# Attention logits of two graph layers kept in their PSUM bank: leaky ReLU in place, running maximum and subtraction from PSUM

## The chip, the cores and the metric

The kernel runs on one core of one Trainium2 chip, as one program. The metric is the device time of one execution in microseconds (us). Its engines are PE (TensorE, matrix products), DVE (VectorE), ACT (ScalarE), POOL (GpSimd) and SP (SyncE), each with an instruction queue of its own that it works off in order; they meet only at semaphores.

## What is computed

The reference is a graph network over 6250 nodes and 106250 edges, sorted by destination, in float32: a layer with a message sum, one with a mean, a GATv2 attention layer with a feed-forward part, and a block of two GAT layers (4 heads of 32 channels, then 1 head of 128). The change touches only the edge work of the last two:

```
def _gat_conv(x, edge_index, W, att_src, att_dst, bias, heads, out_ch, concat):
    h = (x @ W).reshape(N, heads, out_ch)
    a_src = jnp.einsum('nhc,hc->nh', h, att_src)
    a_dst = jnp.einsum('nhc,hc->nh', h, att_dst)
    e = a_src[src] + a_dst[dst]
    e = jnp.where(e > 0, e, NEG_SLOPE * e)          # NEG_SLOPE = 0.2
    m = jax.ops.segment_max(e, dst, num_segments=N)
    e = jnp.exp(e - m[dst])
    s = jax.ops.segment_sum(e, dst, num_segments=N)
    alpha = e / (s[dst] + 1e-16)
    out = jax.ops.segment_sum(h[src] * alpha[:, :, None], dst, num_segments=N)
```

## The kernel before, in words

The three attention layers run through one function, `soft_sweep`, called with layer 2 (GATv2), 3 (first GAT layer, H = 4 heads) and 4 (second GAT layer, H = 1). In it `full` is true for layer 2 alone; what stands under `not full` is layers 3 and 4, which are the fourth and fifth graph layers of the network. The edges are padded to G = 208 groups of GE = 512 edges (four pieces of 128). Four groups make a batch (BATCH = 4), so a layer has 52 batches. In a batch the logits stand as lanes: one partition for each head and group, L = 4H, so 16 partitions by 512 edges in layer 3 and 4 by 512 in layer 4.

What happens to a batch, in order:

- POOL (L1766) gathers the source rows of each piece with one indirect DMA: 832 in a layer, in a plain unrolled loop. It waits only for the message of 16 groups before (AROUND = 16). Each reads its 128 row numbers from the SBUF tile `sources`.
- ACT (L1780) takes the source parts of the logits from the gathered rows; PE sums destination parts (`dst_logits`, L1864) and source parts (`src_logits`, L1870) in `lane_bank`, one of two PSUM banks by the batch's parity.
- ACT (L1822) copies `lane_bank` to the SBUF tile `lanes`.
- DVE, `running_max`: L1980 makes the leaky ReLU, max(0.2 x bank, lanes), into `lanes`. L1983 is the forward running maximum, a scan over `starts` (added; a large negative number where a new destination begins) and the logits. L1987 takes its end, and L1989 scans backward over `starts` and `running`.
- DVE, `carry_on` and, one step later, `shift_lanes`: the maximum is carried across groups by way of PE (L1897, L1913); L2010 joins it into `running`, and L2012 subtracts `running` from the logits into `lanes`.
- ACT (L1810) takes the exponential; PE (L1920) turns the weights round into `weights_bank`; DVE (L2021) multiplies rows by weights; PE (L1880) scatters the messages with one-hot matrices into a window of 64 nodes, which DVE adds to the sums (L1972, L1974).

`sweep16` writes out the same list of steps for every engine, 16 groups to a loop body, and `t.back(k)` is the group k steps behind: a batch's weights are used LAG = 7 steps after its last group's first step began. A wait `wait_ge(sem, n)` holds the engine until the semaphore has reached n; `g.uses(BATCH)` is the number of the batch of group g, from one. On PE, the wait on `weights_lane` before L1920 stands in the step of `t.back(BATCH + 2)`, and the wait on `leaky` that the change replaces stands in `dst_logits`, in front of the first write to a `lane_bank` (j == 1).

Of the kernel before, what the change touches and what calls it, by code (L numbers as in the profile page):

```python
# [21 lines left out]
ALU = mybir.AluOpType  # L22
# [10 lines left out]
GE = TPG * P  # L33
# [8 lines left out]
BATCH = 4  # L42
# [8 lines left out]
AROUND = 16  # L51
NEG = -3.0e38
# [9 lines left out]
def sems(nc, phase, *names, **slots):  # L62

    lists = {n: [nc.alloc_semaphore(f"{phase}_{n}{k}") for k in range(count)] for n, count in slots.items()}
    return named(**{n: nc.alloc_semaphore(f"{phase}_{n}") for n in names}, **lists)
# [8 lines left out]
def settle(eng):  # L74

    eng.nop(nofuse=True)
# [1549 lines left out]
def soft_sweep(nc, io, sb, layer):  # L1626
# [3 lines left out]
    full = layer == 2  # L1630
# [12 lines left out]
    s = sems(nc, phase, *names, gathered=AROUND, attr=AHEAD, dst_rows=DST, onehotT=4, onehot=4)  # L1643

    with ExitStack() as ctx:
        def tile(name, shape, dt=F32):
            return ctx.enter_context(nc.sbuf_tensor(f"{phase}_{name}", shape, dt))[:]
# [6 lines left out]
        starts = tile("starts", [L, GE + 1])  # L1654
        cont = tile("cont", [L, GE])
        lanes = tile("lanes", [L, GE])
        running = tile("running", [L, GE])
# [20 lines left out]
        lane_bank = [sb.psum[0:L, 2 if full else k, :] for k in range(2)]  # L1678
# [20 lines left out]
        def pair(g):  # L1699
            return g.slot(8) // 2  # L1700

        with nc.Block() as block:  # L1702
# [129 lines left out]
            def _(pe):  # L1832
# [22 lines left out]
                def dst_logits(g):  # L1855
                    j = g.slot(BATCH)
                    pe.wait_ge(s.dst_rows[j], g.uses(BATCH, 16))
                    if g.slot(2) == 0:
                        return
                    pe.wait_ge(s.onehotT[pair(g)], g.uses(8, 16))  # L1860
                    if j == 1 and g.back(AROUND + 1).exists():
                        pe.wait_ge(s.leaky, g.back(AROUND + 1).uses(BATCH))
                    settle(pe)
                    pe.matmul(lane_bank[g.half()], dst_cols[:, j // 2], onehotT[:, pair(g)], start=j == 1, stop=False).then_inc(s.edge_term, 2)  # L1864

# [24 lines left out]
                def step(t):  # L1890
                    if t.exists():
                        (edge_terms if full else dst_logits)(t)
# [42 lines left out]
            def _(v):  # L1935
# [40 lines left out]
                def running_max(g):  # L1976
                    n = g.uses(BATCH)
                    v.wait_ge(s.lanes_out, n)
                    if not full:
                        v.scalar_tensor_tensor(lanes, lane_bank[g.half()], 0.2, lanes, ALU.mult, ALU.max).then_inc(s.leaky, 1)  # L1980
                        v.wait_ge(s.leaky, n)
                    v.wait_ge(s.starts_in, g.uses(BATCH, 16))
                    v.tensor_tensor_scan(running, starts[:, 0:GE], lanes, NEG, ALU.add, ALU.max).then_inc(s.running, 1)  # L1983
                    v.wait_ge(s.running, n)
                    if g.back(BATCH).exists():
                        v.wait_ge(s.carry_psum, g.back(BATCH).uses(BATCH))
                    v.tensor_scalar(fend, mask, running[:, GE - 1:GE], None, ALU.mult).then_inc(s.fend, 1)  # L1987
                    v.wait_ge(s.fend, n)
                    v.tensor_tensor_scan(running[:, ::-1], starts[:, GE:0:-1], running[:, ::-1], NEG, ALU.add, ALU.max).then_inc(s.backward, 1)  # L1989
# [13 lines left out]
                def shift_lanes(g):  # L2003
                    n = g.uses(BATCH)
                    v.wait_ge(s.init_psum, n)
                    v.tensor_copy(init, init_bank).then_inc(s.init, 1)
                    v.wait_ge(s.init, n)
                    v.wait_ge(s.backward, n)
                    v.wait_ge(s.cont_in, g.uses(BATCH, 16))
                    v.scalar_tensor_tensor(running, cont, init, running, ALU.add, ALU.max).then_inc(s.maxima, 1)  # L2010
                    v.wait_ge(s.maxima, n)
                    v.tensor_tensor(lanes, lanes, running, ALU.subtract).then_inc(s.shifted, 1)  # L2012
                    if g.back(BATCH).exists():
                        v.wait_ge(s.factor, g.back(BATCH).uses(BATCH))
                    v.tensor_scalar(growth, init, running[:, 0:1], 0.0, ALU.subtract, ALU.min).then_inc(s.factor_log, 1)
# [10 lines left out]
                def step(t):  # L2026
                    g = t.back(1)
                    if g.exists() and full:
                        v.wait_ge(s.z, g.times(1, 1))
                        v.scalar_tensor_tensor(z[:, g.slot(2)], z[:, g.slot(2)], 0.2, z[:, g.slot(2)], ALU.mult, ALU.max).then_inc(s.leaky, 1)  # L2030
                    g = t.back(LAG)
                    if g.closes(0):
                        q = g.half()
                        v.wait_ge(s.factor_psum, g.uses(BATCH))
                        v.tensor_copy(factor_of[:, q], factor_bank).then_inc(s.factor_out, 1)
                        v.tensor_copy(factor_head[:, q], factor_head_bank).then_inc(s.factor_out, 1)
                    if t.back(LAG + 1).exists():
                        add(t, t.back(LAG + 1))
                    if g.exists():
                        weigh(g)  # L2040
                    if t.back(BATCH + 1).closes(0):
                        running_max(t.back(BATCH + 1))
                    if t.back(BATCH + 2).closes(0):
                        shift_lanes(t.back(BATCH + 2))
                    g = t
                    if g.exists() and full:
                        v.wait_ge(s.edge_term, g.times(1, 1))
                        v.wait_ge(s.rows_out, g.times(1, 1))
                        v.tensor_tensor(z[:, g.slot(2)], term_bank, z[:, g.slot(2)], ALU.add).then_inc(s.z, 1)
                    if t.back(BATCH + 1).closes(0):  # L2050
                        carry_on(t.back(BATCH + 1))

                    if nodes:
                        nodes.dve_steps(v, t)
# [786 lines left out]
```

## Time and profile before

| | us |
|---|---|
| median of three runs (lowest, highest) | 6062.57 (6051.43, 6064.77) |
| the profiled execution | 6063.81 |
| its span in the trace | 6061.7 |
| PE busy | 4558.7 |
| POOL busy | 4033.9 |
| DVE busy | 2673.3 |
| ACT busy | 1391.0 |
| first and last gather of layer 3 issued at | 3799.8 and 4880.0 |
| first and last gather of layer 4 issued at | 4943.0 and 6008.9 |

The three runs lie within 13.3 us, 0.2% of the time. All positions are microseconds from the start of the span. The two layers of the change take the stretch from about 3800 to the end.

### The profile page before, as it was taken

The page shows a single profiled execution, that of the slowest core. Times are in us where ns is not written, and L with a number is a line of the kernel's source. Part 1 is how long each engine was busy: PE and PEld are TensorE (multiplying, and loading weights), DVE is VectorE, ACT ScalarE, POOL GpSimd, SP SyncE. Part 2 cuts the span into 40 slices and gives each one's busy share as a digit, 9 for nine tenths or more (in the row PEclk, how much of TensorE's full clock was granted, in tenths as well). Part 3 has the DMA queues.
Part 4 walks back from the last instruction along what each step waited for, and adds up shares of the span by engine and source line. Part 5 has one row for each costly group of instructions (what it writes and reads, how often), then busy time and mean ns, then how long its engine had stood idle before and what let it go on. Part 6 is the DMA issues. An engine that isn't in the chain of part 4 may idle for free. (4 is left out here: it accounts for less than half of the span.)

```text
span 6061.7 us, 88001 instructions
## 1 busy us (share of the span) xinstructions
PE 4558.7 (75%) x19879; PEld 2993.3 (49%) x19879; DVE 2673.3 (44%) x8236; ACT 1391.0 (23%) x4039; POOL 4033.9 (67%) x4164
## 2 busy tenths in 40 slices
PE   3788888647777776999999877577777756776666
PEld 2777777535565563444444455344444434444443
DVE  3222222221111113777777644455555545555555
ACT  2111111221222221222222255122222211222121
POOL 2777777447777775777777400777777747777775
PEclk9999999985555556999999967666676756667666
DMA  4333333244444443555555300445545524444442
GB/s 121 105 105 105 104 104 105 67 137 104 114 115 113 113 105 102 165 165 163 166 164 165 112 10 13 99 107 111 110 110 110 110 66 104 109 105 108 107 107 75
DMA packets 561737, 663.45 MB, mean 109 GB/s; under 512 B 197133, under 2 KB 392590, under 8 KB 560639
## 3 DMA queue, kind: packets, MB, share of 16 engines
q1 hardware_dynamic: 428351, 385.27, 21.5%
q0 software_dynamic: 133120, 275.45, 19.9%
q14 instruction: 199, 1.63, 0.1%
q8 instruction: 67, 1.10, 0.1%
HBM read 580.89 MB, written 86.19 MB: 110 GB/s over the span
## 5 line engine op out<-in xcount | busy, mean ns | idle before, releaser
L1766 POOL DMA_INDIRECT soft_rows<-table,sources x2496 | 2457.7, 985 | 1248.2 <-issue 1243.9
L1880 PE MATMUL psum<-soft_message,soft_onehot 128*64 128x136 f32 (+2 forms) x4992 | 948.0, 350 | 373.6 <-DVE soft_message L2021 200.0
L1880 PEld LDWEIGHTS psum<-soft_message,soft_onehot 128*64 128x64 f32 x4992 | 753.7, 177 | 805.9 <-issue 600.0
L1399 POOL DMA_INDIRECT sum_rows<-table,sources x832 | 785.4, 944 | 373.5 <-issue 369.8
L1069 POOL DMA_INDIRECT term_rows<-table,sources x832 | 790.7, 950 | 354.1 <-issue 354.1
L1806 ACT ACTIVATE soft_window<-psum 64x136 f32<-64x136 f32 (+2 forms) x624 | 171.5, 275 | 1885.1 <-PE psum L1880 1885.1
L1100 PE MATMUL psum<-term_onehot,term_term 128*128 128x64 f32 x1664 | 403.7, 424 | 188.5 <-DVE sums L1152 178.9
L1441 PE MATMUL psum<-sum_onehot,sum_rows 128*128 128x64 f32 x1664 | 358.0, 389 | 221.0 <-DMA sum_rows<-table,sources 220.1
L1100 PEld LDWEIGHTS psum<-term_onehot,term_term 128*128 128x128 f32 x1664 | 370.5, 328 | 242.1 <-issue 241.9
L1441 PEld LDWEIGHTS psum<-sum_onehot,sum_rows 128*128 128x128 f32 x1664 | 341.5, 302 | 274.7 <-issue 270.5
L1146 DVE TENSOR_TENSOR term_term<-psum,term_rows 128x512 f32<-128x512 f32 x208 | 143.8, 691 | 753.1 <-issue 371.1
L1972 DVE TENSOR_TENSOR sums<-sums,psum 128x64 f32 x624 | 136.7, 219 | 763.8 <-PE psum L1888 752.9
L1090 PE MATMUL psum<-L_We,term_attrs 64*128 64x128 f32 x1664 | 430.5, 437 | 8.9 <-DMA term_attrs<-in_ea64T 8.9
L2021 DVE TENSOR_TENSOR soft_message<-soft_rows,psum 128x512 f32<-128x512 f32 x624 | 417.8, 670 | 0.2 <-issue 0.2
L1090 PEld LDWEIGHTS psum<-L_We,term_attrs 64*128 64x128 f32 x1664 | 369.9, 325 | 57.1 <-issue 28.7
L1864 PE MATMUL psum<-soft_onehotT,soft_dst_cols 128*16 128x512 f32 (+1 forms) x416 | 321.9, 869 | 54.6 <-DMA soft_dst_cols<-adst 54.6
L1078 ACT ACTIVATE term_term<-term_term 128x512 f32<-128x512 f32 x208 | 130.9, 630 | 905.0 <-DVE term_term L1146 905.0
L1887 PEld LDWEIGHTS psum<-ident,soft_window 64*128 64x128 f32 x624 | 94.3, 151 | 462.6 <-issue 462.6
L1418 ACT ACTIVATE sum_flat<-psum 64x512 f32<-64x512 f32 x208 | 122.9, 591 | 825.7 <-PE psum L1431 822.1
L1480 DVE TENSOR_TENSOR sums<-sums,psum 128x64 f32 x208 | 46.1, 222 | 581.8 <-PE psum L1442 577.3
L1887 PE MATMUL psum<-ident,soft_window 64*128 64x64 f32 x624 | 182.0, 292 | 158.9 <-ACT soft_window L1806 158.4
L1846 PE MATMUL psum<-soft_onehotT,soft_dst_rows 64*128 64x512 f32 x416 | 235.9, 647 | 0.0
(239 smaller groups left out, 6576.6 us busy)
## 6 DMA issues: line engine op xcount, KB each, us to landing
soft_onehotT<-onehotsT SPq DMA_DIRECT2D x312, 256.0 KB
soft_onehot<-onehots SPq DMA_DIRECT2D x624, 128.0 KB
soft_attrs<-in_ea128T SPq DMA_DIRECT2D x208, 256.0 KB
soft_rows<-table,sources POOLq DMA_INDIRECT x2496
term_attrs<-in_ea64T SPq DMA_DIRECT2D x208, 128.0 KB
onehots<-term_onehot SPq DMA_DIRECT2D x208, 128.0 KB
sum_onehot<-onehots SPq DMA_DIRECT2D x208, 128.0 KB
onehotsT<-sum_flat SPq DMA_DIRECT2D x208, 128.0 KB
```

The lines of the kernel that those rows point to most:

```text
L1069: pool.indirect_dma_start(rows[:, k, t, :], None, io.table0[0:NCH * CN], bass.IndirectOffsetOnAxis(sb.sources[:, g * TPG + t:g * TPG + t + ...
L1090: last = pe.matmul(term_bank[g.slot(4)][:, piece(b)], attrs[:, g.slot(AHEAD), piece(b)], sb.L0_We, start=True, stop=True)
L1100: last = pe.matmul(window[q], term[:, g.slot(4), b, :], onehot[:, g.slot(8), b], start=b == 0, stop=b == TPG - 1)
L1399: pool.indirect_dma_start(rows[:, k, t, :], None, io.table1[0:NCH * CN], bass.IndirectOffsetOnAxis(sb.sources[:, g * TPG + t:g * TPG + t + ...
L1441: pe.matmul(window[q], rows[:, g.slot(AROUND), b, 0:D], onehot[:, k, b], start=b == 0, stop=b == TPG - 1)
L1766: pool.indirect_dma_start(rows[:, k, t, :], None, table[0:NCH * CN], bass.IndirectOffsetOnAxis(sb.sources[:, g * TPG + t:g * TPG + t + 1], ...
L1806: act.activation(window, window_bank, ACT.Copy).then_inc(s.window_copied, 1)
L1846: pe.matmul(term_bank, dst_rows[side(g), k], onehotT[side(g), pair(g)], start=False, stop=True).then_inc(s.edge_term, 1)
L1864: pe.matmul(lane_bank[g.half()], dst_cols[:, j // 2], onehotT[:, pair(g)], start=j == 1, stop=False).then_inc(s.edge_term, 2)
L1880: last = pe.matmul(window_bank, onehot[:, k, b], message[:, g.slot(2), b, :], start=b == 0, stop=b == TPG - 1)
L1887: pe.transpose(window_T[:, 0:W], window[:, 0:D], sb.ident[0:W, 0:W])
L2021: v.tensor_tensor(message[:, g.slot(2), :, 0:D].rearrange("p t (h c) -> p t h c", h=H), rows[:, g.slot(AROUND), :, 0:D].rearrange("p t (h ...
```

## The change

Three DVE instructions of a batch change their operands in layers 3 and 4, and one PE wait is put on another semaphore. Layer 2 is issued as before.

- L1980 writes its result over its PSUM input, `lane_bank`, in place of the SBUF tile `lanes`, which it still reads as its second input.
- L1983 reads the logits from `lane_bank` in place of `lanes`; `starts` stays in SBUF.
- L2012 reads the logits from `lane_bank` in place of `lanes`; `running` stays in SBUF, and so does its output.
- The bank is now read until the subtraction. `dst_logits` waits, before it writes to it anew, for the subtraction (`shifted`) of the batch two before, where it waited for the leaky ReLU of the batch four before.

```
-                    if j == 1 and g.back(AROUND + 1).exists():
-                        pe.wait_ge(s.leaky, g.back(AROUND + 1).uses(BATCH))
+                    if j == 1 and g.back(2 * BATCH).exists():
+                        pe.wait_ge(s.shifted, g.back(2 * BATCH).uses(BATCH))
...
+                    logits = lanes if full else lane_bank[g.half()]
                     if not full:
-                        v.scalar_tensor_tensor(lanes, lane_bank[g.half()], 0.2, lanes, ALU.mult, ALU.max).then_inc(s.leaky, 1)
+                        v.scalar_tensor_tensor(logits, logits, 0.2, lanes, ALU.mult, ALU.max).then_inc(s.leaky, 1)
                         v.wait_ge(s.leaky, n)
                     v.wait_ge(s.starts_in, g.uses(BATCH, 16))
-                    v.tensor_tensor_scan(running, starts[:, 0:GE], lanes, NEG, ALU.add, ALU.max).then_inc(s.running, 1)
+                    v.tensor_tensor_scan(running, starts[:, 0:GE], logits, NEG, ALU.add, ALU.max).then_inc(s.running, 1)
...
-                    v.tensor_tensor(lanes, lanes, running, ALU.subtract).then_inc(s.shifted, 1)
+                    v.tensor_tensor(lanes, lanes if full else lane_bank[g.half()], running, ALU.subtract).then_inc(s.shifted, 1)
```

## Rows read from the trace of the kernel before

**Rows 1.** The page, part 1: busy us (share of the span) and instructions
```profile
PE 4558.7 (75%) x19879; PEld 2993.3 (49%) x19879; DVE 2673.3 (44%) x8236; ACT 1391.0 (23%) x4039; POOL 4033.9 (67%) x4164
```

**Rows 2.** The page, part 4: the chain that ended last, by engine
```profile
POOL 13%; issue 4%; PE 0%; DVE 0%; ACT 0%; DMA 0%; POOLq 0%; DVEq 0%; ACTq 0%
```

**Rows 3.** Busy time of L1766 in layers 3 and 4: stretch, us, POOL busy (instructions)
```profile
core 0: us, POOL busy (x), PEclk, DMA share, GB/s
3795.00:4885.00 1090.00, 827.81 (x832) 0.66 0.48 108
4940.00:6011.00 1071.00, 813.65 (x832) 0.68 0.42 106
```

**Rows 4.** Line L1766, first of layer 3, then of layer 4: ns min/median/max, idle before it
```profile
L1766 POOL DMA_INDIRECT soft_rows<-table,sources x832: 940/944/1841, 3799.8 to 4880.0; - x167
...
  DVE soft_message L2021: 0.6, 2
...
L1766 POOL DMA_INDIRECT soft_rows<-table,sources x832: 940/944/1835, 4943.0 to 6008.9; - x167
...
  issue: 315.3, 832
```

**Rows 5.** DVE instructions of a batch by shape: busy us, mean ns, idle before
```profile
L2021 DVE TENSOR_TENSOR soft_message<-soft_rows,psum 128x512 f32<-128x512 f32 x624 | 417.8, 670 | 0.2 <-issue 0.2
L2030 DVE SCALAR_TENSOR_TENSOR soft_z<-soft_z 128x512 f32<-128x512 f32 x208 | 142.8, 687 | 31.0 <-issue 26.1
L1989 DVE TENSOR_TENSOR_SCAN soft_running<-soft_starts,soft_running 16x512 f32<-16x512 f32 x52 | 63.0, 1212 | 1.8
L1983 DVE TENSOR_TENSOR_SCAN soft_running<-soft_starts,soft_lanes 16x512 f32<-16x512 f32 x52 | 63.0, 1212 | 5.2 <-DMA soft_starts<-lane_starts 0.3
L2012 DVE TENSOR_TENSOR soft_lanes<-soft_lanes,soft_running 16x512 f32<-16x512 f32 x52 | 35.3, 679 | 1.8
L1980 DVE SCALAR_TENSOR_TENSOR soft_lanes<-psum,soft_lanes 16x512 f32<-16x512 f32 x52 | 35.0, 672 | 12.5 <-ACT soft_lanes L1822 12.5
```

**Rows 6.** Timeline, one batch of layer 3: start us, us, engine, line [idle before]
```profile
4079.64 0.67 DVE L1980 SCALAR_TENSOR_TENSOR soft_lanes<-psum,soft_lanes 16x512 f32<-16x512 f32 x1
...
4080.35 1.21 DVE L1983 TENSOR_TENSOR_SCAN soft_running<-soft_starts,soft_lanes 16x512 f32<-16x512 f32 x1
4080.52 1.79 POOL L1766 DMA_INDIRECT soft_rows<-table,sources  x1 [0.30 <-issue]
...
4081.84 1.21 DVE L1989 TENSOR_TENSOR_SCAN soft_running<-soft_starts,soft_running 16x512 f32<-16x512 f32 x1
4082.62 1.19 POOL L1766 DMA_INDIRECT soft_rows<-table,sources  x1 [0.31 <-issue]
...
4085.10 0.74 DVE L2010 SCALAR_TENSOR_TENSOR soft_running<-soft_cont,soft_init,soft_running 16x512 f32<-16x512 f32 x1
4085.37 1.29 POOL L1766 DMA_INDIRECT soft_rows<-table,sources  x1 [0.30 <-issue]
4085.87 0.68 DVE L2012 TENSOR_TENSOR soft_lanes<-soft_lanes,soft_running 16x512 f32<-16x512 f32 x1
```

**Rows 7.** Timeline, two batches of layer 4, the same columns
```profile
5013.65 1.21 DVE L1983 TENSOR_TENSOR_SCAN soft_running<-soft_starts,soft_lanes 4x512 f32<-4x512 f32 x1
5013.78 1.83 POOL L1766 DMA_INDIRECT soft_rows<-table,sources  x1 [0.30 <-issue]
...
5198.71 0.94 POOL L1766 DMA_INDIRECT soft_rows<-table,sources  x1 [0.30 <-issue]
5198.74 1.23 DVE L1983 TENSOR_TENSOR_SCAN soft_running<-soft_starts,soft_lanes 4x512 f32<-4x512 f32 x1
5199.96 0.95 POOL L1766 DMA_INDIRECT soft_rows<-table,sources  x1 [0.30 <-issue]
5200.25 1.21 DVE L1989 TENSOR_TENSOR_SCAN soft_running<-soft_starts,soft_running 4x512 f32<-4x512 f32 x1
5201.22 1.00 POOL L1766 DMA_INDIRECT soft_rows<-table,sources  x1 [0.30 <-issue]
```

## The prediction

> **What bounds the kernel now.** I began with the page's busy line: PE has most (75%), DVE less than half, POOL two thirds [rows 1]. That line mixes nine stages, so I went to the chain that ended last. It is POOL's: 13% of the span, with the sequencer's issue time as the only other share over 0% [rows 2]. Then line L1766 by layer. In layer 4 POOL issues 832 gathers from 4943.0 to 6008.9 and stands idle 315.3 us before them, all of it "issue", most of it in the fixed 0.30 us between two gathers; in layer 3 only 0.6 us of its idle time ends at another engine (DVE's message) [rows 4, 6]. So layers 3 and 4 last as long as POOL takes to issue: nothing that PE, ACT or DVE saves is worth anything there unless POOL gets faster by it. The reader is to see in rows 4 that the median gather takes 944 ns and the longest 1841 and 1835. At 944 ns, 832 take 785.4 us; they took 827.8 and 813.7 [rows 3]. POOL loses 42.4 us in layer 3 and 28.2 us in layer 4, 70.6 us together. The change can only be worth a part of that, or add to it.
>
> **Where POOL loses it.** The timeline with POOL and DVE side by side answers this. A gather that starts at 4080.52 takes 1.79 instead of 0.94, held by 0.85; the scan L1983 runs from 4080.35 to 4081.56, 1.04 after the gather's start. The next one is held 0.25, and L1989 ends 0.43 after its start. At 5013.78 it is 0.89 held and 1.08 to the scan's end, at 5201.22 0.06 and 0.24 [rows 6, 7]. The difference is 0.18 to 0.19 each time: a gather has one moment, 0.185 us after its start, at which it can't go on while such a DVE instruction runs, and it waits for that instruction's end. Call it the gather's read. Under L2010 the wait lasts 0.06 longer than the instruction (held 0.35, end at 0.47) [rows 6]. A read up to 0.16 us after a scan's start still slips through (5198.71), one 0.32 after it is held (5013.78) [rows 7]; I take 0.24 for the edge, with those two as its bounds.
>
> I went through all gathers and DVE instructions of the stretch from 3840 in this way. L1983 holds 75 of them, 26.5 us in total; L1989 101, 23.9 us; L2010 101, 18.6 us. That is 69.0 of the 70.6 us. These have two tensor inputs in SBUF. Reads that fall into L2021 (198 of them, one input in PSUM) or L1980 (52, one in PSUM) are not held at all. L2012 has two SBUF inputs but holds none: L2010 ends 0.03 before it starts and has just let a read through, and the next comes 1.2 us later, when L2012 is over [rows 6].
>
> The Trainium skill has this rule (SBUF — State Buffer, Who interferes with whom): a DVE instruction with two SBUF inputs contends with a GpSimd instruction that reads SBUF, one with at most one SBUF input does not. The held gathers agree. It also says that whoever comes second is blocked, DVE included; here the scans last 1212 ns in the mean whether or not they meet a gather, so that half is not seen.
>
> **The change, part by part.**
>
> *L1983 reads the logits from PSUM.* It keeps one SBUF input, as L2021 and L1980 have, so I take it that it no longer holds POOL. Its 26.5 us do not come back, though. Reads are 0.94 + 0.30 = 1.245 us apart, and L1989 starts 1.49 after L1983 [rows 6]. Say a read falls r after L1983's start. Before: held until 1.21, its next read is at 1.21 + 1.245 = 2.455, inside L1989 (1.49 to 2.70), held 0.25; in total 2.70 - 1.245 - r. After: it passes, the next read is at r + 1.245, inside L1989, held until 2.70: again 2.70 - 1.245 - r. The hold only moves from the first scan to the second. The exception is an r so small that r + 1.245 falls before L1989's edge, 1.49 + 0.24 = 1.73, so r under 0.49: then that read passes, the next at r + 2.49 comes after L1989's end, and the batch saves nearly all. Between the edge at 0.24 and 0.49 I find 12 of 104 batches, the first at 4080.52 (0.85 and 0.25 held, [rows 6]) and the last at 5013.78 (0.89 held, [rows 7]); ten of them in layer 3. Each saves its two holds, 1.0 to 1.15, and on the average 0.1 more at L2010. Laid over every batch's own positions, this gives 41.1 us of holds before and 29.3 after in layer 3, 28.5 and 26.0 in layer 4: 11.8 + 2.5 = 14.3 us saved. Check: in layer 3 the r are spread evenly over 1.245, so (0.49 - 0.24)/1.245 = 20% of 52 batches, 10.4 by 1.15 = 12.0. In layer 4 they cluster: most scans begin 0.03 to 0.5 after a gather's start, as at 5198.74, so few have a small positive r. With the edge at 0.16 the window ends at 0.41 and has 6 batches (7 us), with 0.32 it ends at 0.57 and has 16 (19 us): 7 to 19.
>
> *The durations.* They matter only through the position of L1989 and L2010 against the reads. With an input in PSUM the same kinds take 670 (L2021) and 672 (L1980) ns, all in SBUF 679 (L2012) and 687 (L2030) [rows 5]. So reading PSUM costs between -15 and 0 ns; a scan with a large PSUM input isn't in the trace, nor is any DVE write to PSUM. Bounds for these: 0.02 to 0.05 less each, from those pairs, and at the other end a second pass over 512 elements if reading and writing one bank exclude each other, which I put at half a scan's 1212 ns, 0.6 us. I take 0 to -0.05, as the PSUM rows lie there. With everything 0.05 earlier the positions give 30.5 and 23.5, a saving of 15.6; 0.1 later 25.8 and 31.1, 12.7.
>
> The Trainium skill speaks against the change here (VectorE: DVE Perf Modes, on the TRN2 errata): its fixed cost is 120 cycles from PSUM and 58 from SBUF. With L1983 longer by that difference, an estimate of 0.065 us at the page's 0.96 GHz, the saving would be 12 us. The rows show no such cost [rows 5].
>
> *L1980 writes to PSUM, L2012 reads from it.* L1980 held nothing and holds nothing. L2012 held nothing, so freeing it brings 0. Should L2010 stop standing in front of it, its place is worth no more than what L2010 takes now, 18.6 us. ACT still copies the bank first, so no instruction goes or comes on any queue.
>
> *The PE wait.* It asks for the subtraction of the batch two before, later than the old one. But PE has waited on `weights_lane` of the same batch three steps earlier (t.back(6) at step 4b - 2, this at 4b + 1), and ACT issues that only after `shifted`. So it is met when PE arrives, cost 0. If it were not, all of PE's scatters stand behind it; they have a gather's lead of 16 groups before POOL waits, so it would cost nothing on POOL either until PE were some 80 us late (16 groups of 1066/208 us).
>
> *Ends.* After the last gather of each layer some 53 to 58 us drain through all engines, with one such DVE chain in it: 0.1 us at most.
>
> **Sum.** 6063.8 (profiled execution) - 14.3 = 6049.5; against the median, 6062.6 - 14.3 = 6048.3. What no change looks like here is about 0.2%, 12 us.
>
> **Rivals.**
> 1. *The scan holds POOL still*, because the scan form itself takes the way to SBUF. For it: no scan with a PSUM input of size is in the trace. Against: L2010 and L1980 are one kind of instruction, and it is the place of the inputs that divides them. Time 6062.6, give or take 5 for the shift.
> 2. *The hold is gone and nothing takes its place*: if the positions move so that reads fall beside L1989. The whole 26.5 us: 6036. Against: L1989 holds a read that falls anywhere in 0.97 of every 1.245 us; only a shift of L1989 against the reads in most batches does it.
> 3. *Slower: writing over its own PSUM input makes L1980 and L1983 late.* In layer 4 reads sit just before the scan, so each 0.1 us of delay of L1989 adds 5 us, up to 47 us of holds at 0.4 to 0.5 late, against 28.5; layer 3 gives 26 to 30. 47 + 27 - 69.6 = +4, so 6067; together with rival 1 up to 90 us of holds, 6083. It decides from 0.3 us of delay. Against: no PSUM row is slower at all.
>
> **How the numbers follow.** Forecast 0.60, rival 1 0.17, rival 2 0.08, rival 3 0.08; the other 0.07 is drift of positions either way. The forecast's own range, 7 to 19 us and some 6 for the scatter of the runs, is 6039 to 6060; with rivals 1 and 3 the range goes to 6066, with part of 2 down to 6037. Faster by over 0.2% (under 6050.4): six tenths of the forecast, rival 2 and some drift, 0.46. Slower by over 0.2%: 0.09. Same: 0.45.
>
> **What would show it.** Gathers that meet L1983 take 0.94; those that meet L1989 are held more than 0.25, up to 0.97, in layer 3, their total near 22 us there and 15 in layer 4; L2010 near 18 in both. L1766 is busy 816 and 811. L1980, L1983 and L2012 last within 0.05 of before; no PE idle time ends at L2012. Wrong if L1983's gathers still take over 1.0, if L1766's busy time falls by over 20 us, or if the stretches change while it does not.

## The result, and the profile after

The changed kernel takes 6046.6 us (median of 12 runs, 6042.0 to 6059.6) where the kernel before takes 6058.1 (12 runs, 6051.4 to 6068.5): ratio 0.9981, 95% interval 0.9972 to 0.9989, so 11.5 us less, 7 to 17. The forecast was 14.3 less, 6048.3 us. The profiled execution has a span of 6040.0 us.

The page's busy lines and the chain's first line, which compare with [rows 1, 2]:

```profile
PE 4546.9 (75%) x19879; PEld 2977.6 (49%) x19879; DVE 2675.0 (44%) x8236; ACT 1390.2 (23%) x4039; POOL 4021.5 (67%) x4164
```

```profile
POOL 13%; issue 4%; PE 1%; DVE 0%; DMA 0%; ACT 0%; POOLq 0%; DVEq 0%; ACTq 0%
```

POOL still sets the end. The busy time of L1766, layer 3 in the first stretch and layer 4 in the second, compares with [rows 3]; the columns are stretch, us, POOL busy (instructions), granted clock, DMA share, GB/s:

```profile
3700.00:4880.00 1180.00, 813.65 (x832) 0.65 0.44 101
4910.00:6060.00 1150.00, 815.26 (x832) 0.68 0.39 99
```

Layer 3 lost 14.2 us of holds (827.8 to 813.7) and layer 4 gained 1.6 (813.7 to 815.3). The first and last starts of L1766 say the same of the stretches (as in [rows 4]):

```profile
L1766 POOL DMA_INDIRECT soft_rows<-table,sources x832: 940/944/1902, 3790.4 to 4856.4; - x167
...
L1766 POOL DMA_INDIRECT soft_rows<-table,sources x832: 940/944/1902, 4919.2 to 5986.8; - x167
```

Layer 3's gathers last 1066.0 us instead of 1080.2, layer 4's 1067.6 instead of 1065.9, and the drains behind them are as before (62.8 and 53.2 us against 63.0 and 52.8). The span fell by 21.7 us; 9.4 of it is the start of layer 3, at 3790.4 instead of 3799.8, before the change can act. That start lies anywhere from 3787 to 3802 in the ten traces whose kernels took 6020 to 6070 us, whatever the kernel, and is scatter. The change's own part in this pair of traces is 12.3 us.

The DVE instructions, against [rows 5]:

```profile
L1990 DVE TENSOR_TENSOR_SCAN soft_running<-soft_starts,soft_running 16x512 f32<-16x512 f32 x52 | 63.1, 1214 | 1.8
L1984 DVE TENSOR_TENSOR_SCAN soft_running<-soft_starts,psum 16x512 f32<-16x512 f32 x52 | 62.8, 1208 | 5.0
L1981 DVE SCALAR_TENSOR_TENSOR psum<-psum,soft_lanes 16x512 f32<-16x512 f32 x52 | 35.4, 680 | 13.1 <-ACT soft_lanes L1822 13.1
L2013 DVE TENSOR_TENSOR soft_lanes<-psum,soft_running 16x512 f32<-16x512 f32 x52 | 35.3, 678 | 1.8
```

(L1981, L1984, L1990 and L2013 are L1980, L1983, L1989 and L2012 of before, one or so lines on.) The in-place write costs 8 ns more, the scan from PSUM 4 less, the subtraction 1 less.

And the place where it happens, two batches of layer 3 in the timeline (compare [rows 6]):

```profile
3859.98 1.21 DVE L1984 TENSOR_TENSOR_SCAN soft_running<-soft_starts,psum 16x512 f32<-16x512 f32 x1
3860.29 0.94 POOL L1766 DMA_INDIRECT soft_rows<-table,sources  x1 [0.30 <-issue]
3861.47 1.21 DVE L1990 TENSOR_TENSOR_SCAN soft_running<-soft_starts,soft_running 16x512 f32<-16x512 f32 x1
3861.54 1.90 POOL L1766 DMA_INDIRECT soft_rows<-table,sources  x1 [0.30 <-issue]
...
4130.99 1.21 DVE L1984 TENSOR_TENSOR_SCAN soft_running<-soft_starts,psum 16x512 f32<-16x512 f32 x1
4131.23 0.94 POOL L1766 DMA_INDIRECT soft_rows<-table,sources  x1 [0.30 <-issue]
4132.47 0.94 POOL L1766 DMA_INDIRECT soft_rows<-table,sources  x1 [0.30 <-issue]
4132.49 1.23 DVE L1990 TENSOR_TENSOR_SCAN soft_running<-soft_starts,soft_running 16x512 f32<-16x512 f32 x1
4133.72 0.94 POOL L1766 DMA_INDIRECT soft_rows<-table,sources  x1 [0.30 <-issue]
```

Both halves of the argument can be seen here. A gather's read is taken 0.185 us after its start, as in the prediction. The gather at 3860.29 reads 0.49 us into the forward scan and takes 0.94: it would have been held before. But the next one is caught by the backward scan and held 0.96. At 4131.23 the read comes 0.43 into the scan, the next comes 0.17 us after the backward scan's start, the third after its end, and none is held. (The backward scan itself takes 1.23 there and not 1.21; the last section comes back to that.)

The table goes through all gathers from 3840 on in this way. Each cell has the reads that fell into an instruction, how many of these were held, and the us of hold in all:

| kernel, layer | forward scan | backward scan | join | all holds |
|---|---|---|---|---|
| before, 3 | 48, 40, 20.2 | 50, 50, 11.8 | 50, 50, 8.4 | 40.4 |
| after, 3 | 48, 0, 0 | 50, 34, 20.6 | 43, 42, 7.3 | 27.0 |
| before, 4 | 46, 35, 6.1 | 51, 51, 11.7 | 51, 51, 10.0 | 27.5 |
| after, 4 | 44, 0, 0 | 51, 48, 19.6 | 51, 51, 9.9 | 29.2 |

Of the 26.3 us that the forward scan gave up, 16.7 came back under the backward scan. What the forecast asked to see is there: held by the backward scan 20.6 and 19.6 us (22 and 15 expected), by the join 17.2 (18), busy time 813.7 and 815.3 (816 and 811).

### The profile page after: what moved, and what is told of

Read it like the earlier page. It is cut to its first block and busy times, and to the rows that moved or that the text cites. A ratio compares the mean times of both kernels' runs of the same rounds, so it can differ in the third digit from the quotient of the medians.

```text
span 6040.0 us, 87969 instructions
## 1 busy us (share of the span) xinstructions
PE 4546.9 (75%) x19879; PEld 2977.6 (49%) x19879; DVE 2675.0 (44%) x8236; ACT 1390.2 (23%) x4039; POOL 4021.5 (67%) x4164
## 5 line engine op out<-in xcount | busy, mean ns | idle before, releaser
L1766 POOL DMA_INDIRECT soft_rows<-table,sources x2496 | 2444.9, 980 | 1238.3 <-issue 1232.5
L1399 POOL DMA_INDIRECT sum_rows<-table,sources x832 | 785.4, 944 | 373.8 <-issue 368.0
L1864 PE MATMUL psum<-soft_onehotT,soft_dst_cols 128*16 128x512 f32 (+1 forms) x416 | 329.3, 888 | 54.5 <-DMA soft_dst_cols<-adst 54.5
```

The source lines that it names most:

```text
L1399: pool.indirect_dma_start(rows[:, k, t, :], None, io.table1[0:NCH * CN], bass.IndirectOffsetOnAxis(sb.sources[:, g * TPG + t:g * TPG + t + ...
L1766: pool.indirect_dma_start(rows[:, k, t, :], None, table[0:NCH * CN], bass.IndirectOffsetOnAxis(sb.sources[:, g * TPG + t:g * TPG + t + 1], ...
```

## The experiments

Each was timed beside the kernel before on the same chip. That took 6057.4 us beside scan_from_sbuf, fwd_alone_holds, all_one_input and layer2_too, and 6059.7 beside sub_from_sbuf, old_wait, late_half and late_most. Ratios are to that, with 95% intervals. Diffs are against the changed kernel (that of before_one_scatter against the kernel before); `...` in a line of code stands for arguments left out.

**scan_from_sbuf.**

```
-                    v.tensor_tensor_scan(running, starts[:, 0:GE], logits, NEG, ...)
+                    v.tensor_tensor_scan(running, starts[:, 0:GE], lanes, NEG, ...)
-                        v.scalar_tensor_tensor(logits, logits, 0.2, lanes, ...)
+                        v.scalar_tensor_tensor(logits, logits, 1.0, lanes, ...)
```

> The changed kernel with one operand put back: the forward scan reads its logits from the SBUF tile again; the in-place write to PSUM and the subtraction from PSUM stay. The leaky factor is 1.0 in layers 3 and 4, so that both copies hold the same numbers; the leaky ReLU is left out of the result. Theory (the place of the scan's second input decides whether it holds the gathers): reads that fall into the forward scan are held again, 25 to 35 us in all; the busy time of the gathers in layers 3 and 4 is back at 820 to 830 and 810 to 820 us; time within 6 us of the kernel before, 6058. Rival (the gain comes from the write to PSUM or from the subtraction): 6047, as the changed kernel.

Measured: 6058.1 us, ratio 1.0004 (0.9995 to 1.0013). Busy time of the gathers in layers 3 and 4:

```profile
3700.00:4880.00 1180.00, 822.90 (x832) 0.65 0.45 101
4910.00:6060.00 1150.00, 813.87 (x832) 0.67 0.40 100
```

The forward scan holds 38 and 32 gathers again, 25.1 us in all. One operand takes the whole gain away; the write to PSUM and the subtraction from it together bring nothing.

**sub_from_sbuf.**

```
-                    v.tensor_tensor(lanes, lanes if full else lane_bank[g.half()], running, ALU.subtract)
+                    v.tensor_tensor(lanes, lanes, running, ALU.subtract)
```

> The changed kernel with the subtraction reading the SBUF tile again, which holds the raw logits there, so the leaky ReLU is left out of the weights; forward scan and in-place write stay in PSUM. Theory: the subtraction held no gather before and none now: the time of the changed kernel, 6047 within 6; gathers under the forward scan take 0.94. Rival (part of the gain is the subtraction's): over 6052.

Measured: 6045.8 us, 0.9977 (0.9966 to 0.9987): as the changed kernel. Seven reads fell into the subtraction, which has two SBUF inputs here, all of them 0.03 to 0.13 us after its start, and none was held: they came before the edge. So its operands' place is worth nothing in this kernel, because of where the reads fall. That it can hold a gather is shown once, in layer 2 of layer2_too: a read 0.61 us into the subtraction from SBUF, and that gather takes 1.07.

**old_wait.**

```
-                    if j == 1 and g.back(2 * BATCH).exists():
-                        pe.wait_ge(s.shifted, g.back(2 * BATCH).uses(BATCH))
+                    if j == 1 and g.back(AROUND + 1).exists():
+                        pe.wait_ge(s.leaky, g.back(AROUND + 1).uses(BATCH))
```

> The changed kernel with PE's old wait (leaky ReLU of the batch four before) in place of the new one (subtraction of the batch two before). Theory: the new wait is always met, so the time is the changed kernel's, 6047 within 6, and PE's idle time before the first write to a bank is the same. Rival (the wait costs PE something that the shorter holds hide): under 6043.

Measured: 6045.5 us, 0.9976 (0.9964 to 0.9988). PE's wait costs nothing. In the changed kernel's trace PE's idle time before L1864 ends at "issue" (68.9 us; before 66.8) and at the transfer of `soft_dst_cols` (54.5; before 54.6), never at the subtraction.

**fwd_alone_holds.**

```
+        edge_max = [running if full else sb.psum[32:32 + L, k, :] for k in range(2)]
-                    v.tensor_tensor_scan(running, starts[:, 0:GE], logits, ...)
+                    v.tensor_tensor_scan(edge_max[g.half()], starts[:, 0:GE], lanes, ...)
-                    v.tensor_tensor_scan(running[:, ::-1], starts[:, GE:0:-1], running[:, ::-1], ...)
+                    v.tensor_tensor_scan(edge_max[g.half()][:, ::-1], starts[:, GE:0:-1], edge_max[g.half()][:, ::-1], ...)
-                    v.scalar_tensor_tensor(running, cont, init, running, ALU.add, ALU.max)
+                    v.scalar_tensor_tensor(running, cont, init, edge_max[g.half()], ALU.add, ALU.max)
```

L1988 also reads the maximum's end from `edge_max`, and the leaky factor is 1.0 in layers 3 and 4, as in scan_from_sbuf.

> The mirror image of the change: forward scan reads SBUF twice and holds, but it writes to a second PSUM region, from which the backward scan and the join read, so that these two have one SBUF input. Leaky factor 1.0 in layers 3 and 4 (leaky ReLU left out). Theory, by the positions in the changed kernel's trace: only the forward scan's holds are left, about 23 us in layer 3 and 11 in layer 4 of the 69 us; 6058 - 36 = 6022, between 6014 and 6030. Rival (a fixed sum of holds is passed on to whatever dual-SBUF work is left): no better than the changed kernel, 6047.

Measured: 6039.7 us, 0.9972 (0.9959 to 0.9984), so 17 us less than before and not 36. None of the 101 reads in the backward scan and none of the 100 in the join is held; the forward scan holds 91 gathers, 42.2 us. Layer 3 came out as worked out (gathers 1061.9 us long against 1062 by the positions); in layer 4 the scans no longer sat just behind a read, and the forward scan held 21.2 us there and not 11. The cause of the holds is confirmed, the forecast of positions is not. Some of what the chain freed was also taken up by small instructions of the node steps with two SBUF inputs (L1543 and L1559), which hold 6 us here and under 1.5 in the kernel before.

**all_one_input.** The same, but the forward scan reads `logits` (in PSUM in layers 3 and 4) as in the changed kernel, and the factor is 0.2.

> The changed kernel, and in layers 3 and 4 the forward and the backward scan write to PSUM (partitions 32 and up of the lane bank) and the join reads from there into SBUF, so that no large instruction of the chain has two SBUF inputs. Whole computation kept. Theory: all holds by the chain go, nothing to take over; gathers of layers 3 and 4 busy 786 to 790 us each; of 69 us of holds before 67 to 69 are saved: 5990, between 5984 and 5997. Rival (POOL is held by another engine's or the DMA's traffic and the scans only mark the time): 6040 to 6047.

Measured: 6029.2 us, 0.9961 (0.9947 to 0.9974): the fastest of the kernels that compute everything, level with layer2_too, 24 us under before by the ratio (16 to 32), and far from the 67 expected. Its gathers (the first fence: busy by layer; the second, for layer 4: first and last start, and what ended POOL's idle time):

```profile
3700.00:4880.00 1180.00, 786.88 (x832) 0.66 0.45 101
4910.00:6060.00 1150.00, 786.96 (x832) 0.66 0.40 99
```

```profile
L1767 POOL DMA_INDIRECT soft_rows<-table,sources x832: 940/945/1298, 4918.5 to 5957.8; - x167
...
  issue: 328.7, 815
  DVE soft_message L2023: 5.2, 17
```

The holds are gone but for 1.5 us in each layer: 41 us less busy time in layer 3, 27 in layer 4, and layer 4's gathers last 1039.3 us. So 67.6 us were won on POOL. Of these, 40 were given back in the drains: from the last gather of layer 3 (4836.9) to the first of layer 4 it takes 81.6 us instead of 63.0, and from 5957.8 to the span's end at 6032.1 74.3 instead of 52.8. The chain of waits between 5000 and 5900 shows who sets the pace, first in the kernel before, then in this one:

```profile
by line: POOL soft_rows L1766 76.3%; issue 23.8%
```

```profile
by line: PE psum L1881 28.2%; issue 14.5%; DVE soft_message L2023 9.9%; PE psum L1871 8.1%; DVE psum L1985 6.0%; PE psum L1865 6.0%; PE psum L1888 4.2%; DVE psum L1982 3.4%; ACT soft_window L1807 2.7%; PE psum L1921 2.6%; PE psum L1927 2.1%
```

Before, POOL alone. Now the scatter (L1881), the message (L2023) and what joins them. In the same stretch POOL's line has 72.7% of the chain in the changed kernel and 48.4% in fwd_alone_holds, so the change of hands is gradual. The reading that fits: POOL has become faster than the loop of PE, DVE and ACT behind it, runs up to its lead of 16 groups (16 x 1039/208 = 80 us, beside drains of 81.6 and 74.3) and waits for a message now and then. Over the two layers this loop had only the 24 to 28 us of room that the kernel gained. This is argued from the chain and the drains; the experiments that were to test it, the last four below, could not.

**layer2_too.** The same for layer 2's backward scan and join (`edge_max` in bank 2 there).

> The kernel of all_one_input, with the same for layer 2's backward scan and join; its forward scan still has two SBUF inputs. In layer 2 the gathers lose about 30 us to holds too, but PE is busy over 90% of the stretch and POOL already waits for messages now and then. Theory: the holds there fall to about 10 us, and PE's pace takes what is won: 0 to 12 us under all_one_input, 5984. Rival (layer 2 is bound by POOL alone): 20 us under it, 5970.

Measured: 6029.9 us, 0.9963 (0.9949 to 0.9976), no different from all_one_input. Layer 2's gathers run from 2354.6 to 3422.1, 1067.5 us, where the kernel before has 1068.6 (2355.4 to 3424.0). But the condition of the test was not met. The holds in layer 2 did not fall to 10 us; the gathers' busy time there, this kernel first and then the kernel before, hardly moved:

```profile
2300.00:3500.00 1200.00, 815.20 (x832) 0.95 0.51 150
```

```profile
2300.00:3500.00 1200.00, 816.19 (x832) 0.95 0.51 150
```

The backward scan holds none of its 50 reads any more (50 held, 12.3 us, in all_one_input). They now land in L2032, layer 2's leaky ReLU over the SBUF tile `soft_z`, which has two SBUF inputs as well: it holds 54 gathers, 15.0 us, where in all_one_input it held 6, 1.5 us. One of them:

```profile
2412.23 1.22 DVE L1991 TENSOR_TENSOR_SCAN psum<-soft_starts,psum 32x512 f32<-32x512 f32 x1
2412.99 0.94 POOL L1767 DMA_INDIRECT soft_rows<-table,sources  x1 [0.30 <-issue]
...
2415.19 0.67 DVE L2032 SCALAR_TENSOR_TENSOR soft_z<-soft_z 128x512 f32<-128x512 f32 x1
2415.49 1.20 POOL L1767 DMA_INDIRECT soft_rows<-table,sources  x1 [0.30 <-issue]
```

So this is the change's own effect once more, a hold passed on to the next instruction of its kind, here in full. Whether POOL's holds bound layer 2 stays open.

**late_half, late_most.** One and two memsets of 0.42 us each on DVE in layer 4, between leaky ReLU and forward scan:

```
+                        if layer == 4:
+                            v.memset(pad, 0.0).then_inc(s.late, 1)
+                            v.wait_ge(s.late, g.uses(BATCH, 2) - 1)   # late_most only
+                            v.memset(pad, 0.0).then_inc(s.late, 1)    # late_most only
```

> The changed kernel; in layer 4 alone a memset of about 0.43 us (no inputs, so it holds nothing) stands on DVE between the leaky ReLU and the forward scan, so that both scans and what follows come later. Theory (only the position of the backward scan against the gathers' reads decides): by the positions in the changed kernel's trace layer 4's holds go from 30 to about 40 us; its gathers last 1077 us instead of 1067.6, layer 3 stays at 1066 within 5; time 6057. Rival (DVE has slack and positions don't matter): 6047, layer 4 at 1067.

> As late_half, with two memsets, about 0.9 us in all. Theory: the backward scan now mostly falls between reads; layer 4's holds go from 30 to about 16 us, its gathers last 1053 us although DVE has 47 us more to do. Time 6033 if POOL alone sets layer 4; the kernel with all inputs apart gained only 7 us on this one in layer 4 with its end, since PE, ACT and DVE then drained later, so rather 6040. Rival (later is worse): layer 4 over 1077, time over 6057.

Measured: late_half 6061.9 us, 0.9997 (0.9987 to 1.0007); late_most 6053.2, 0.9984 (0.9975 to 0.9992). Busy time of the gathers in layer 4, late_half first:

```profile
4900.00:6060.00 1160.00, 821.52 (x832) 0.64 0.39 99
```

```profile
4900.00:6060.00 1160.00, 814.16 (x832) 0.66 0.39 99
```

late_half went as forecast: in layer 4 the gathers are busy 822 us against 815 in the changed kernel and last 1073.9 against 1067.6, the drain behind them is 57.6 us against 53.2, and the gain of the change is gone. late_most was not worth the 14 us; its layer 4 is as the changed kernel's (1066.1 us). Its scans begin at all distances from a gather's start (2, 14, 11, 6 and 18 of 51 per quarter of a microsecond) instead of mostly near 0.3: the added work loosened the locking that the forecast rested on. Twice the delay hurts less than once, which says that position counts, and not the amount of DVE work alone. The profiled executions are not typical ones: late_half's was the slowest of its 12 (6070.6 us) and late_most's the second fastest (6040.6), so the statement rests on the medians and the busy times. Why the scans lock to the gathers in layer 4 is open.

**before_one_scatter, after_one_scatter, all_one_scatter, all_one_scatter_again.** The kernel before, the changed kernel and all_one_input (this one twice), each with one of four scatter products in layers 3 and 4 (the `stop` flag of the product follows):

```
-                    for b in range(TPG):
+                    for b in range(TPG if full else 1):
```

> The kernel before with less work for PE: in layers 3 and 4 only the first of a group's four scatter matrix products is issued, so three quarters of the messages are left out of the sums. Theory (POOL's gathers set these layers before the change): nothing but the drains changes, gathers of layers 3 and 4 last 1080 and 1066 us within 6, time 6050 to 6058. Rival (PE sets part of the pace already): under 6040.

> The changed kernel with the same three of four scatter products left out in layers 3 and 4. Theory: POOL still sets the pace in the changed kernel and holds decide, so 10 to 20 us under the kernel before with one scatter product; holds by the backward scan 30 to 45 us in all, none by the forward scan. Rival (the changed kernel was capped by PE, ACT and DVE): 30 us or more under it.

> The kernel in which no large chain instruction has two SBUF inputs, with the same scatter products left out. Theory (there the missing 40 us of gain were taken by PE's, ACT's and DVE's own pace, of which the scatter is a large part): gathers 1039 us per layer, the drains after them back at 53 to 63 us instead of 74 and 82; about 65 us under the kernel before with one scatter product, 5985 to 5995. Rival (something else, as the gathers' landing, makes the drains long): still 28 us under it, drains of 74 and 82.

> The kernel of all_one_scatter once more, since the chip of that call ran every kernel 1.6 ms slower, with SP's one-hot transfers late, and so told nothing here. Theory: with three of four scatter products left out in layers 3 and 4, PE, ACT and DVE keep up with gathers of 1039 us per layer, drains are back at 53 to 63 us, and the whole 68 us of holds is won: 5990 where the kernel before takes 6058. Rival (the drains are not PE's): 6029, drains of 74 and 82.

Measured: 7577, 7578, 7601 and 7624 us. The kernel before took 7675 us beside the first three and 7692 beside the last: on these two chips everything is a quarter slower, for a reason that the traces don't give. There other waits decide. Two lines on the last kernel (who waited for whom, us in all, times, longest):

```profile
POOL soft_rows L1767 <- DVE soft_message L2023: 999.3, 309, 23.1
ACT soft_window L1807 <- DMA soft_onehot<-onehots: 566.9, 64, 21.5
```

POOL waits a millisecond for messages, and among what ACT waits for are the one-hot transfers. None of the expected differences appeared: the changed kernel is level with the one before, and all_one_scatter is 24 us longer than before_one_scatter. In before_one_scatter too POOL waits 892 us for messages, so its holds are not what sets the time there. Nothing follows for the question, and that a lighter scatter would give back the 40 us of drains is not shown.

## Why the prediction was right, and where it was not

- *POOL bounds layers 3 and 4, by holds.* Right, and shown: with the holds gone (all_one_input) the gathers are busy 786.9 us in each layer, beside 785.4 for 832 median gathers, and the time falls; but only its first 24 to 28 us do so.
- *Two large SBUF inputs hold a gather at its read, one does not.* Right, shown in both directions: 92 reads in the forward scan from PSUM, none held; 70 held when its input is put back (scan_from_sbuf); 101 in the backward scan from PSUM, none held (fwd_alone_holds). Rival 1 falls. All of these that don't hold have their other input in PSUM. A small instruction with a single SBUF input and none in PSUM does hold: L1545 (tensor_scalar, 128x256, 0.29 us) held 10 gathers in the ten traces, all with reads 0.24 us or more after its start, and let 20 pass, all at 0.23 or less. The rule quoted from the Trainium skill (SBUF — State Buffer, Who interferes with whom) agrees with the scans; it leaves the 2-port perf modes out of what it says on one SBUF input, and whether L1545 runs in one no run here shows.
- *"That half is not seen"*, that VectorE is blocked when it comes second. Wrong: the scan waits too, up to 0.08 us, as the last section shows; the mean of 1212 ns hid it. The cost of it is small, and the forecast did not rest on it.
- *The hold moves to the backward scan.* Right: 16.7 of 26.3 us moved. Rival 2, the full 26.5 us, falls. In the after-trace's layer 3 a read 0.48 into the forward scan led to no hold (4743.88), and one 0.49 did (3860.29); the edge had been worked out as 0.49.
- *Its size by layer.* Layer 3 was sized at 11.8 us and measured 14.2 in the pair of profiles; layer 4 was sized at 2.5 and measured -1.7. Both are positions drawn anew: in layer 3 of the four other traces in which the scan has these operands (sub_from_sbuf, old_wait, late_half, late_most) the gathers last 1066.1 to 1072.8 us, and in layer 4 of the first two 1062.6 and 1064.0. With the changed kernel's own, the means are 1068.8 and 1064.7; before and scan_from_sbuf average 1077.7 and 1066.1. That gives 8.9 and 1.4, 10.3 us in all, beside 11.5 from the clock. The term was some 3 us too high, well inside its own 7 to 19. That the time itself came within 2 us (6048.3 forecast, 6046.6 measured) is luck: the kernel before, at 6062.6 in three runs, takes 6058.1 over twelve, and the two misses cancel. The working by positions is also less sure than this one hit suggests: with it fwd_alone_holds was put at 36 us and gave 17, and late_most at 1053 us of gathers in layer 4 and gave 1066.
- *Durations.* I took 0 to -0.05 us. The scan is 0.004 shorter, the in-place write 0.008 longer: for the write the sign was off, the size too small to matter. The Trainium skill's rule that PSUM costs DVE more (VectorE: DVE Perf Modes, on the TRN2 errata) is not borne out at 0.065 us. Rival 3's premise falls, though late_half shows that its mechanism is real: 0.4 us of lateness in layer 4 costs the whole gain. Its price was too high: it put 47 us of holds on layer 4, and there late_half has 36 (821.5 - 785.4).
- *The subtraction and PE's wait at 0.* Right, by sub_from_sbuf and old_wait.
- *Not foreseen, in the experiments:* that the engines behind POOL had only 24 to 28 us of room. The prediction of the change didn't need it, the forecast for all_one_input did.

## What to carry to other kernels

Where GpSimd issues gathers back to back, look in the timeline for gathers that take longer than the median and for the VectorE instruction they end with; moving one of its two SBUF inputs to PSUM frees the gather, here at a cost to VectorE of -4 to 8 ns an instruction. A hold taken away from one instruction can be caught by the next of the same kind, one gather period on: most of it was in this change, and all of it in layer2_too. So count what remains by positions, or free all of them at once, and look over every VectorE instruction of the stretch for it. Before pricing that, see how long the engines behind need from the last gather: that is where the next bound shows.

## What the runs showed that I had not expected

- The held gather's read is sharp to about 0.01 us: 0.185 us after its start, held until the scan's end, until 0.06 after it for the join and the other instructions that are not scans. A read in a scan's first 0.23 us slips through; from 0.23 to 0.25 on, it is held (one at 0.25 in layer 2 of the kernel before). A small tensor-tensor instruction of the node steps with two SBUF inputs (L1543, 0.43 us) behaves alike: reads up to 0.22 into it pass, those from 0.25 are held. The edge is not the same everywhere: right behind the message, L1559 held gathers with reads 0.11 to 0.20 after its start (six in three traces) and one scan of layer 2 held one at 0.16 (fwd_alone_holds).
- VectorE waits as well. A scan that reads two tensors from SBUF and writes there takes 1.204 to 1.215 us as a rule. When a read slips through 0.15 to 0.23 us after its start it takes longer, by 1 ns for each ns that the read comes after 0.147, up to 1.293. In the ten traces 39 such scans take over 1.215, all as this line says within 3 ns, and none without such a read does. Scans with one input in PSUM don't wait: 21 forward scans had a read at these positions, and none took over 1.209. [rows 7] has one of the first kind, 1.23 at 5198.74. This one, in layer 3 of the changed kernel, has both kinds; the reads come 0.48 and 0.23 us after the scans' starts:

```profile
4743.59 1.21 DVE L1984 TENSOR_TENSOR_SCAN soft_running<-soft_starts,psum 16x512 f32<-16x512 f32 x1
4743.88 0.94 POOL L1766 DMA_INDIRECT soft_rows<-table,sources  x1 [0.30 <-issue]
...
4745.09 1.29 DVE L1990 TENSOR_TENSOR_SCAN soft_running<-soft_starts,soft_running 16x512 f32<-16x512 f32 x1
4745.13 0.95 POOL L1766 DMA_INDIRECT soft_rows<-table,sources  x1 [0.30 <-issue]
```

- Writing its result to PSUM costs the scan 9 to 16 ns (1221 and 1225 in all_one_input, 1224 to 1228 in fwd_alone_holds, against 1212). L1988, the small instruction that takes the maximum's end, goes from 217 ns to 268 in all_one_input. Reading that [L, 1] scalar from PSUM is not the whole cause: it does so in fwd_alone_holds too and takes 225, and in the changed kernel, where the scalar is in SBUF and only the scan before it reads PSUM, it takes 228. Why the two together cost 50 is open.
